# Feed-forward rows started at the first step of the second attention block, with the second matrix staged in other rooms

## The reference, cut to what matters

```python
def attn(x, Wq, Wkv, Wout):               # 16 heads of 64, 4 groups of keys and values
    xn = layernorm(layernorm(x)) * ln_scale + ln_bias
    q, (k, v) = xn @ Wq, split(xn @ Wkv)
    q, k = layernorm(q), layernorm(k)     # over the 64 of a head
    out = softmax(q @ k.T * 64 ** -0.5) @ v
    return out @ Wout
def bitlinear(x, w):                      # 8-bit activations, ternary weights
    s = mean(abs(w)); wq = clip(round(w / s), -1, 1) * s
    a = 127 / max(abs(x), axis=-1);  xq = round(x * a) / a
    return xq @ wq.T
def ffn(x): return bitlinear(gelu(bitlinear(x, w1)), w2)   # 1024 -> 4096 -> 1024
x = x + attn(x)
x = x + ffn(layernorm(x))
```

## Time and profile before

| what | value |
|---|---|
| time, median of 3 runs | 2154.29 us (2152.71 to 2158.37) |
| the profiled execution | 2159.15 us, span of its slowest core 2157.6 us |
| spans of its eight cores | 2144.6 to 2157.6 us, mean granted clock 0.951 to 0.954 |
| busy share of the span | PE 87%, ACT 66%, DVE 56%, POOL 6% |
| block 0, block 1, block 2 (slowest core) | start at 159.2, 398.6, 641.2 us |
| blocks 2 to 6, block 7, tail | 221 us each, 209 us, 203 us |

### The profile page before, as it was taken

One profiled execution on the slowest core, in us unless ns is written; L12 is line 12 of the kernel. 1 busy time (PEld: TensorE's weight loads), 2 busy tenths in 40 slices (PEclk: granted clock), 3 DMA queues, 4 the chain that ended last, 5 costly groups with the idle time before them and its releaser, 6 DMA issues.

```text
span 2157.6 us, 42477 instructions; the slowest of 8 cores (2144.6 to 2157.6 us)
## 1 busy us (share of the span) xinstructions
PE 1869.8 (87%) x16196; PEld 891.9 (41%) x16196; DVE 1201.2 (56%) x1725; ACT 1416.3 (66%) x1466; POOL 127.7 (6%) x109
## 2 busy tenths in 40 slices
PE   3645667667999999999999999999999999998897
PEld 2213333333444444444444444444445444444343
DVE  5445888775535554464556446554555545445663
ACT  6457767556677777777777777777777787773120
POOL 0420012100000100010000000000000000000000
PEclk9777789778999999999999999999999999999999
DMA  9499754550322232423233322332233232222412
GB/s 295 125 304 336 260 185 157 176 166 17 69 64 58 79 77 45 95 82 94 45 74 103 94 45 69 108 92 48 69 108 89 45 74 55 50 45 69 98 39 69
DMA packets 235142, 225.27 MB, mean 104 GB/s; under 512 B 203328, under 2 KB 203584, under 8 KB 227136
## 3 DMA queue, kind: packets, MB, share of 16 engines
q1 hardware_dynamic: 234944, 222.56, 37.8%
HBM read 135.51 MB, written 36.70 MB: 80 GB/s over the span
## 4 chain that ended last, share of the span: by engine, by line
PE 61%; ACT 12%; DVE 12%; issue 10%; DMA 4%; POOL 1%; SPq 1%; DVEq 0%; ACTq 0%; POOLq 0%
PE PA L875 16%; PE PA L886 14%; PE PS L779 9%; PE PV L795 9%; ACT P L921 6%; PE PA L846 4%; PE PA L865 4%; DMA X<-x 3%; PE PA L819 2%; ACT H L929 2%; ACT L931 1%; DVE s_tmp L1244 1%; DVE HQ L1260 1%; ACT HQ L951 1%; ACT L926 1%
## 5 line engine op out<-in xcount | busy, mean ns | idle before, releaser
L921 ACT ACTIVATE P<-PS,s_nbnd 128x1024 bf16<-128x1024 f32 x1024 | 1078.1, 1113 | 395.8 <-PE PS L779 395.5
L875 PE MATMUL PA<-W,YB 128*128 128x512 fp8e4 x2048 | 484.9, 382 | 11.8 <-DVE H L1237 7.6
L886 PE MATMUL PA<-W,HT 128*128 128x512 fp8e4 x1984 | 459.8, 379 | 0.0
L779 PE MATMUL PS<-QB,K 64*128 64x512 bf16 x2048 | 337.7, 393 | 108.7 <-ACT P L921 106.3
L795 PEld LDWEIGHTS PV<-V,P 128*128 128x128 bf16 x8192 | 304.9, 99 | 196.1 <-issue 142.9
L795 PE MATMUL PV<-V,P 128*128 128x65 bf16 x8192 | 344.7, 196 | 37.1 <-DVE AO L1078 37.1
L1237 DVE TENSOR_SCALAR H<-PA,s_c 128x512 f32<-128x512 f32 x256 | 190.7, 749 | 329.5 <-PE PA L875 329.4
L875 PEld LDWEIGHTS PA<-W,YB 128*128 128x128 bf16 x2048 | 184.8, 98 | 244.3 <-issue 57.5
L886 PEld LDWEIGHTS PA<-W,HT 128*128 128x128 bf16 x1984 | 180.4, 98 | 220.4 <-issue 29.4
L779 PEld LDWEIGHTS PS<-QB,K 64*128 64x128 bf16 x2048 | 71.9, 94 | 276.4 <-issue 263.9
L929 ACT ACTIVATE H<-H 128x2048 f32<-128x2048 f32 x64 | 118.7, 1902 | 71.8 <-DVE H L1237 71.6
(11 more groups left out here) (120 smaller groups left out, 1198.0 us busy)
## 6 DMA issues: line engine op xcount, KB each, us to landing
X<-x SPq DMA_DIRECT2D x56, 512.0 KB, 5.2
W<-w1t SPq DMA_DIRECT2D x18, 1024.0 KB, 11.8
y<-X SPq DMA_DIRECT2D x32, 512.0 KB, 3.1
H<-w2t SPq DMA_DIRECT2D x14, 1024.0 KB, 11.0
WR<-scr_wo SPq DMA_DIRECT2D x6, 2048.0 KB, 8.1
W<-w2t SPq DMA_DIRECT2D x10, 1024.0 KB, 22.0
WR<-scr_wq SPq DMA_DIRECT2D x5, 2048.0 KB, 9.7
H<-w1t SPq DMA_DIRECT2D x8, 1024.0 KB, 15.6
```

The source lines that it names most:

```text
L779: ins = q.matmul(out=PS[:, i % 2, 512 * r:512 * r + 512], lhsT=K[64 * r:64 * r + 64, s, pr, 128 * kt:128 * kt + 128], rhs=QBc[p % 2][64 * ...
L875: ins = q.matmul(out=o, lhsT=YT[:, c], rhs=W1[:, c, 512 * n:512 * n + 512], start=(c == 0), stop=(c == 7))
L886: ins = q.matmul(out=o, lhsT=HTc[T == NT - 1][:, c], rhs=W2[:, c, 512 * h:512 * h + 512], start=(c == 0), stop=(c == 31))
L921: q.activation(out=P[:, i % 4], in_=PS[:, i % 2], func=AF.Exp, bias=nbnd[:, 0:1], scale=0.125).then_inc(sems["EXP"], 1)
```

## The change

The second matrix's pieces now go into other rooms (`SH_SLOT`): `HT`, three parts of `W2f` (the room of the signs themselves, in parts whose signs come later), and two of the four tiles of `X2`. `H` and `HQ` are free once WT(0, 11) has read them, and F1E waits for that only. Pieces 0, 4, 8, 11, 13 and 15 use `HT`, pieces 7, 10, 12 and 14 the part of `X2`; from piece 10 on these two rooms alternate. The rows of x for tiles 2 and 3 are loaded after WT(1, 14), and HTD(0) waits for WT(1, 15). Block 1 becomes a stage like blocks 2 to 6: WO(0) stands at step 2 instead of 24, F1(0) at steps 7 to 17 instead of 27 to 33, and the eight groups of Q at steps 14 to 25 instead of 1 to 17. `WR` is loaded once more each way. The number of groups, of sign passes and of every other compute instruction in block 1 is the same.

```diff
-SLOTS = {"SG": 6, "SH": 4, "LK": 8, "LX": 4, "LAO": 2, "OUT": 4, "SPL": 4}
+SLOTS = {"SG": 6, "LK": 8, "LX": 4, "LAO": 2, "OUT": 4, "SPL": 4}
-STAGE = {2: 4, 3: 8, 4: 12, 5: 16, 6: 20}
-FIRST = 24
+STAGE = {1: 0, 2: 4, 3: 8, 4: 12, 5: 16, 6: 20}
+SH_SLOT = (0, 1, 2, 3, 0, 1, 2, 4, 0, 1, 4, 0, 4, 0, 4, 0)
+SH_PUT = {55: (0,), 57: (1, 2, 3), 58: (4,), 59: (5,), 60: (6,), 61: (7,), 62: (8,), 63: (9,), 65: (10,), 66: (11,),
+          68: (12,), 69: (13,), 70: (14,), 71: (15,)}
...
-        if 55 <= i < 71:
-            put("sp", "SH", i - 55)
+        for r in SH_PUT.get(i, ()):
+            put("sp", "SH", r)
+        if i == 72:
+            put("sp", "LX", 2)
+            put("sp", "LX", 3)
...
-        if p < 2:
-            jobs += [(0.0, put, "sp", "LXT", p + 1)]
-            jobs += Q(A) + [(0.6, kt, 7)] * (p == 0) + Q(A + 1) + [(0.6, qt, A)] + Q(A + 2) + [(0.6, qt, A + 1)] + Q(A + 3)
-            jobs += [(0.6, qt, A + 2), (0.6, qt, A + 3)]
-            if p == 1:
-                jobs += [(0.0, put, "sp", "WRO", 1), (0.0, lao, 0), (0.0, lao, 1)]
-                jobs += [(0.0, put, "sp", "LX", t) for t in range(4)]
-                jobs += [(0.0, None)]
+        if p == 0:
+            jobs += [(0.0, put, "sp", "LXT", 1)]
+            jobs += Q(A) + [(0.6, kt, 7)] + Q(A + 1) + [(0.6, qt, A)] + Q(A + 2) + [(0.6, qt, A + 1)] + Q(A + 3)
+            jobs += [(0.0, put, "sp", "WRO", 0), (0.6, qt, A + 2), (0.6, qt, A + 3)]
+        if p == 1:
+            jobs += [(0.0, put, "sp", "LX", 0), (0.0, put, "sp", "LX", 1), (0.0, lao, 0), (0.0, lao, 1), gap(4.0)]
...
-    SH = [SG[4], SG[5], HQ.bitcast(F32), HT.bitcast(F32)]
+    SH = [HT.bitcast(F32), SG[3], SG[2], SG[1], X2[:, 2:4].rearrange("p k w -> p (k w)")]
...
-                if T >= 12:
+                if T >= 8:
                     dve.wait_ge("WO", STAGE[T // 4 - 1] + 1, 1)
...
-                dve.wait_ge("WT", 1, 15)
+                dve.wait_ge("WT", 0, 11)
```

More of the change, by code:

```diff
@@ L55, in put @@
     def put(self, engine, kind, *ix):
-        name = kind + (str(ix[-1] % SLOTS[kind]) if kind in SLOTS else "")
+        name = kind + (str(ix[-1] % SLOTS[kind]) if kind in SLOTS else
+                       str(SH_SLOT[ix[-1]]) if kind == "SH" else "")
         self.count[name] = self.count.get(name, 0) + 1
@@ L408, in make_plan @@
                 if stage:
-                    jobs += F1(T)[:6] + Q(A) + F1(T)[6:] + Q(A + 1) + F2(T - 1)[:4]
+                    first, second = (F2(T - 1)[:4], F2(T - 1)[4:]) if T else ([gap(6.0)], [gap(4.0)])
+                    jobs += F1(T)[:6] + Q(A) + F1(T)[6:] + Q(A + 1) + first
                     jobs += [(0.0, ytd, T + 1), (0.6, qt, A)] + Q(A + 2) + [(0.6, qt, A + 1)] + Q(A + 3)
-                    jobs += [(0.0, put, "sp", "WRO", p)] + F2(T - 1)[4:]
+                    jobs += [(0.0, put, "sp", "WRO", p)] + second
                     jobs += [(0.6, qt, A + 2), (0.6, qt, A + 3), (0.0, lao, T + 2)]
@@ L418, in make_plan @@
                     jobs += out
-                if stage:
-                    pass
-                else:
+                if not stage:
                     if T + 2 < NT and T + 2 < 4 * p:
@@ L426, in make_plan @@
                         jobs += F2(T - 1)[:7] + [(0.0, htd, T)] + F2(T - 1)[7:]
-                    elif T:
+                    else:
                         jobs += F2(T - 1)[:4] + tail + F2(T - 1)[4:]
-                    else:
-                        jobs += [gap(6.0)] + tail
                 if T + 1 < NT:
@@ L438, in make_plan @@
         base = (total - (TILES[p][1] - TILES[p][0]) * bonus if 0 < p < NB else total) / 64
[L439 to L442, removed]
         for k in range(64):
@@ L446, in make_plan @@
             pl.flush()
-            if hold and k == FIRST:
-                jobs.pop(hold[0])
-                base, granted = then, spent
             while stream < min(74, pace(64 * p + k)):
@@ L453, in make_plan @@
             granted += base + (bonus if gelu and 0 < p < NB else 0.0)
-            mid = spent if 1 < p and k == 0 else (spent + granted) / 2
+            mid = spent if p and k == 0 else (spent + granted) / 2
             last = k == 63
@@ L460, in make_plan @@
                     put("act", "EXP", kt2)
-            while pos < len(jobs) and jobs[pos][1] and spent + jobs[pos][0] / 2 < mid:
+            while pos < len(jobs) and spent + jobs[pos][0] / 2 < mid:
                 cost, fn, *args = jobs[pos]
@@ L473, in make_plan @@
                             put("sp", "AOS", kt2 // 128)
-            while pos < len(jobs) and jobs[pos][1] and (last or spent + jobs[pos][0] / 2 < granted):
+            while pos < len(jobs) and (last or spent + jobs[pos][0] / 2 < granted):
                 cost, fn, *args = jobs[pos]
@@ L625, in stages @@
     def stages(T):
-        return max([2] + [p + 1 for p in STAGE if STAGE[p] + 2 <= T])
+        return max([1] + [p + 1 for p in STAGE if STAGE[p] + 2 <= T])
     @blk.sync
@@ L666, in _ @@
                 r, = ix
[L667 to L673, removed]
+                was = [k for k in range(r) if SH_SLOT[k] == SH_SLOT[r]]
+                if was:
+                    sp.wait_ge("WT", 1, was[-1])
+                elif r == 0:
                     sp.wait_ge("SPL", 7)
                     sp.wait_ge("KV", 31)
-                q.dma_start(out=SH[r % 4].rearrange("p (c w) -> p c w", w=1024),
+                elif r < 4:
+                    sp.wait_ge("WT", 0, 16 - r)
+                else:
+                    sp.wait_ge("XN", 31)
+                q.dma_start(out=SH[SH_SLOT[r]].rearrange("p (c w) -> p c w", w=1024),
                             in_=w2t_in[256 * r:256 * r + 256].rearrange("(c p) w -> p c w", p=128)
-                            ).then_inc(sems[f"SH{r % 4}"], 16)
+                            ).then_inc(sems[f"SH{SH_SLOT[r]}"], 16)
             elif kind == "LK":
@@ L691, in _ @@
                     sp.wait_ge("XN", 31)
+                    if T >= 2:
+                        sp.wait_ge("WT", 1, 14)
                 q.dma_start(out=X2[:, T % 4], in_=x_in[128 * T:128 * T + 128]).then_inc(sems[f"LX{T % 4}"], 16)
@@ L718, in _ @@
                 else:
-                    sp.wait_ge("SPL", 7)
+                    sp.wait_ge("WT", 1, 15)
                 q.dma_start_transpose(out=HTc[T == NT - 1], in_=HQB).then_inc(sems["HTD"], 16)
@@ L839, in _ @@
                     pe.wait_ge("LXT", p)
-                if p < 3:
+                if p < 2:
                     pe.wait_ge("WQC", 3)
@@ L1326, in _ @@
                     dve.wait_ge("WT", 0, 15)
-                    src = SH[r % 4]
+                    src = SH[SH_SLOT[r]]
                 dst = W1[:, r // 2, 2048 * (r % 2):2048 * (r % 2) + 2048] if m == 0 else \
```

## The result

| kernel | median | ratio to before, 95% interval |
|---|---|---|
| before | 2156.31 us (20 runs) | |
| changed | 2161.68 us (20 runs) | 1.0025 [1.0018, 1.0033] |

The change costs 0.25%, 5.4 us. I had forecast a gain of 4.9 us. The time lies in my range, and inside the 0.3% that I called "same", but the sign is wrong, and the interval is narrow enough to see it.

What follows compares the result with a forecast made beforehand. PE bounds blocks 2 to 6; block 1's first part is a loop of in-order queues with DVE busiest. The terms end block 1 at 636.3 instead of 641.2, 4.9 us less, giving 2149.4 us; range 2135 to 2164.

Steps and rivals of the forecast that it cites:

- Term 1: Block 1, first WO at step 2: DVE idles 10 us for store and load back, until 415.9; maybe 3 more.
- Term 2: Block 1, from the first WO to WT(1, 15): DVE's work is 76 us, ending at 491.9 with no idle.
- Term 3: DVE's idle up to WT(1, 15) in block 1: 13 us, between 4 and 24, so it ends at 504.9.
- second rival: Steps 7 to 22: PE and DVE waits add up as PE's clock falls, making the kernel slower, 2163; chance 0.18.
- My own sign of being wrong: WT(1, 15) ending before 497 or after 512, or the rest of block 1 taking under 124 us.
- Term 4: Block 1 from step 24: 113 us of PE work at a factor of 1.13, 127.7 us; block ends at 636.3.
- The first rival: Block 1: sign pieces and F1 groups fill each other, DVE idle 6 us, rest at 1.05, 2133; chance 0.22.
- The clock: Old first part of block 1: granted clock 0.78, with PE's waits all for ACT or DVE, none for a transfer.
- Edits at nothing: Sign-piece load waits, 0 to 3 us and 0 to 4 at block 0's end, taken as 0; extra `WR` loads covered.

Runs made afterwards that it cites:

- Experiment 4: Changed kernel with x tiles 0 and 1 loaded at the end of block 0 and piece 8 behind LAO(1): ratio 1.0004 to the kernel before.
- experiment 1: Kernel before with only the second matrix's new rooms and their waits, in the old order of jobs: ratio 1.0069 to the kernel before.
- experiment 5: Changed kernel with both repairs (first WO at step 6, no load beside the attention results' store and load back): 2135.72 us, ratio 0.9914 to before.

## Why the prediction was wrong

The working is held against core 6 of the changed kernel, whose block 1 starts 0.6 us later than in the profile of before.

**Term 1, mis-sized: this is the step that failed.** I had 10 us of idle on DVE ahead of the first WOE, at 415.9; it idled 15.3 and the WOE came at 421.9, 5.4 us late after the shift of 0.6. NRM(7) ended as forecast. The store and the load took 8.1 and 7.0 us, where I had 5.6 and 4.4 from block 2. I named the three loads beside it and wrote that they may be "3 more", but left this out of the sum. Experiment 4 shows that they cost block 1 4.3 us, and without them the kernel is level with before (1.0004). That takes away the loss; the gain that I had forecast is not there even then, which is the matter of the base below.

**Term 2, right.** DVE's work from there to WT(1, 15): 76 forecast, 74.5 busy (the row ends with the last sign pass, and DVE does nothing in it before the first WOE at 421.9):

```profile
416.70:509.30 92.60, 67.93 (x577) 32.38 (x582) 74.51 (x81) 51.37 (x54) 5.42 (x2) 0.84 0.43 135
```

**Term 3, right.** From the first WOE at 421.9 to the end of WT(1, 15) at 509.3 are 87.4 us, so 13 of idle, as taken. One of the waits is the one that the second rival describes: NRM(9) behind a stretched sign piece stopped PE for 3.8 us, the next group took 3.6 us, and DVE waited 3.6 for it.

```profile
477.48 1.04 PE L793 MATMUL PV<-V,P 128*128 128x65 bf16 x16 [3.79 <-DVE AO L1076]
478.33 3.60 PE L873 MATMUL PA<-W,YB 128*128 128x512 fp8e4 x8
```

But it did not pile up, and that rival (2163 by a term 3 of 24) did not happen; the time came near it by term 1 instead. My own sign of being wrong, WT(1, 15) outside 497 to 512, did not show the error either: at 509.3 it is inside.

**Term 4, right within 1.3, for a reason that was not there.** 132.7 us from there to block 2, 131.4 forecast. I took the factor of 1.13, "since the start is again at a broken clock". The granted clock of the two stretches from step 24 on was 1.00 and 0.98. What made them long were waits of PE at nearly full clock, 16 us between 509.9 and 642.0:

```profile
PE PS L777 <- ACT P L919: 9.8, 16, 1.0
PE PV L793 <- DVE AO L1076: 4.7, 2, 3.0
PE PA L853 <- DVE QH L1179: 1.7, 1, 1.7
```

The row that the factor came from had a clock of 0.98 itself. It was the right row, taken for a wrong reason, and that it fitted is in part luck.

**The base.** The sum gave a block 1 of 237.7 us. I set it against the 242.6 of the profiled slowest core. Six of the eight cores had 238.4 to 238.9, so even with term 1 as forecast the gain was about 1 us on them, and not 4.9. The per-core spans were there (2144.6 to 2157.6 us); I should have cut block 1 on all cores, which the trace allows. So most of my forecast gain was never there on them. By the error of term 1 alone block 1 would be as long as the 242.6 that I compared with (core 6 has 242.8); the loss shows against the other cores.

**The first rival.** It said that the two halves, DVE's signs and PE's feed-forward, would fill each other, 2133 us. The Trainium skill (Perfetto Trace Analysis, Optimization Strategy) has it that interleaving such regimes may improve performance. The changed kernel does not gain by it (1.0025). The version with both repairs comes to the rival's time, 2135.7 us, but only in part by its way: DVE's idle between the first WOE and the last sign piece is 8.9 us there, 6 in the rival, and from step 24 on the block takes 130.8 us for about 115 us of work (by the prices of term 4, with one group and one QT more), a factor of 1.13 and not 1.05. More than half of the gain is DVE's wait ahead of the first WOE, which the rival had left as it was. I had counted that wait as a fixed price of the change and never asked what it would cost to put the group behind it.

**The clock.** The granted clock in the first two stretches of the changed kernel is 0.71 and 0.84. In the first stand PE's two waits for transfers, 12.5 and 3.2 us. In the second, steps 8 to 24, no wait of PE is for a transfer, the longest is 3.8 us for DVE's normalization, and PE is idle 16.9 of 65.3 us. In the repaired version the same steps have 0.93 with PE idle 19.3 of 68.5 us, so the busy share alone does not tell the clock. The Trainium skill (TensorE: Matmul & The Clock Gate, Loop structure matters more than you think) has it that VectorE's copy out of PSUM does not break PE's warmth where the next group's matmuls follow immediately. Here they do not follow immediately, and no run here tests that case.

**Edits at nothing.** The loads of the sign pieces made none of them wait, and the two more loads of `WR` were hidden, as forecast. But experiment 1 shows that the rooms were not free in themselves: in the old order they hold up SP's queue and cost 9 us. In the changed kernel the load of piece 8, which waits for its room, stands directly ahead of the store AOS(0). It held nothing up: it was issued at 402.0, and the store at 403.0, when NRM(7) had ended (402.9).

## What to carry to other kernels

Before moving a group that needs a store and a load back, ask what its queue could run meanwhile, and put it behind that much work: 4 steps later were worth 16 us of block 1 here, four times what the change itself had cost. Price a transfer from a row with the same neighbours, not from one where it runs alone. A gain on a profiled slowest core is compared with the same stretch on the others first. When a buffer is moved to another room, read the issuing queue: the wait for the new room is paid by whatever stands behind it.

## What the runs showed of the hardware that I had not expected

- A store of 1 MB from SBUF, up to its end as seen by the next issue, took 4.0 to 5.1 us with no load issued near it (experiment 4, eight cores), 5.2 to 6.6 at block 2's start of the kernel before, and 7.7 to 10.9 beside 2 MB of loads. A transposing load landed after 4.4 us (block 2), 5.7 to 7.1 (experiment 4) and 6.8 to 7.1 (the changed kernel).
- The clock stayed at 0.93 in steps with PE busy 72% of the time (experiment 5), and was 0.84 at 74% in the changed kernel. What sets it was not tried.
- A second sign pass takes 2.35 us, and 3.4 to 3.8 where it overlaps with GpSimd squaring a tile of queries: three such passes in block 1 of the kernel before, one in the changed kernel, and no pass without the overlap is stretched.
- Block 1 of one and the same kernel differed between the cores of one execution by 4.8 us (before: 238.4 to 243.2), by 1.8 with both repairs and by 7.5 with the first WO at step 10. Where this comes from is open.
